# Gate and up of experts 3 to 6 as seven block products (Strassen and Winograd's scheme) in a fused attention and expert kernel

## The reference, cut to what matters

```
gate = einsum('btd,edf->ebtf', x, Wg)
up   = einsum('btd,edf->ebtf', x, Wu)
gate, up of the first two experts: plus a low-rank term
mid  = silu(gate) * up
out  = einsum('ebtf,efd->ebtd', mid, Wd)       (low-rank term for the first two)
y    = einsum('bte,ebtd->btd', weights, out)   (weights: a router over the 8 experts)
x    = x + gb * y
```

## Time and profile before

| | |
|---|---|
| time, median of 3 runs | 805.98 us (804.53 to 806.50) |
| the profiled execution's own time | 805.75 us |
| its span, first to last instruction | 804.0 us |
| mean granted clock of PE | 0.998 |
| busy: PE, DVE, ACT, POOL | 793.1, 508.3, 465.8, 403.3 us |
| instructions | 14773 |

### The profile page before, as it was taken

The page is one execution under the profiler, slowest core; times in us unless marked ns, Lnnn a source line. Parts: engine busy times, 40 slices in busy tenths (PEclk is TensorE's granted clock), DMA queues, the critical chain, the costliest instruction groups (busy, mean ns, idle before and its releaser), DMA issues.

```text
span 804.0 us, 14773 instructions
## 1 busy us (share of the span) xinstructions
PE 793.1 (99%) x5116; PEld 710.0 (88%) x5116; DVE 508.3 (63%) x1074; ACT 465.8 (58%) x1259; POOL 403.3 (50%) x547
## 2 busy tenths in 40 slices
PE   9899999999999999999999999999999999999997
PEld 8688899999999999999999999898888888888887
DVE  5667676475466667457557757666785454554575
ACT  5777677677577767767667866652553232332322
POOL 3767587486567567567657656220311010110493
PEclk9999999999999999999999999999999999999999
DMA  9200010000000000000000000202410110100002
GB/s 334 104 28 1 2 61 1 1 8 2 0 8 2 1 4 5 1 2 8 1 1 8 1 1 2 79 1 53 118 40 2 40 40 1 40 0 1 1 1 106
DMA packets 8329, 22.32 MB, mean 28 GB/s; under 512 B 1592, under 2 KB 4280, under 8 KB 8128
## 3 DMA queue, kind: packets, MB, share of 16 engines
q1 hardware_dynamic: 7680, 21.29, 7.9%
q10 hardware_dynamic: 576, 0.08, 0.1%
HBM read 19.26 MB, written 2.11 MB: 27 GB/s over the span
## 4 chain that ended last, share of the span: by engine, by line
PE 94%; DVE 2%; ACT 1%; issue 1%; POOL 1%; DMA 1%; ACTq 0%; DVEq 0%; POOLq 0%
PE ps_o L671 14%; PE ps_proj L548 9%; PE ps_proj L550 9%; PE ps_proj L549 9%; PE ps_s L548 7%; PE ps_s L549 7%; PE ps_s L550 7%; PE ps_turn L600 4%; PE ps_y L548 4%; PE ps_y L549 4%; PE ps_y L550 4%; PE ps_turn L618 3%; PE ps_turn L548 2%; PE ps_turn L549 2%; PE ps_turn L550 2%; PE ps_o L550 2%
## 5 line engine op out<-in xcount | busy, mean ns | idle before, releaser
L671 PE MATMUL ps_o<-vaug,probs 128*128 128x129 f32 x1024 | 136.1, 276 | 1.7 <-POOL probs L1674 0.9
L671 PEld LDWEIGHTS ps_o<-vaug,probs 128*128 128x128 f32 x1024 | 130.0, 192 | 8.0 <-POOL probs L1674 1.4
L993 ACT ACTIVATE ps_s<-ps_s,knorm 128x512 f32<-128x512 f32 x128 | 79.3, 657 | 96.2 <-PE ps_s L550 96.1
L1287 DVE RECIPROCAL rden<-ps_o 128x2 f32<-128x2 f32 x128 | 21.8, 170 | 155.5 <-PE ps_o L671 155.3
L1680 POOL TENSOR_TENSOR we_lo<-raw_e,we_hi 128x512 fp32r<-128x512 f32 x22 | 28.4, 1318 | 161.3 <-ACT we_hi L1036 161.3
L1257 DVE TENSOR_TENSOR prod<-ps_proj,cs 128x1024 f32<-128x1024 f32 x76 | 92.5, 1218 | 11.0 <-ACT sq L936 11.0
L1625 POOL TENSOR_TENSOR root<-ssq,powers 128x4 f32<-128x4 f32 x76 | 77.8, 1024 | 27.4 <-ACT sq L936 27.4
L936 ACT ACTIVATE sq<-ps_proj 128x128 f32<-128x128 f32 x304 | 80.1, 279 | 18.9 <-PE ps_proj L550 16.0
L1641 POOL TENSOR_TENSOR prod<-prod 128x512 f32<-128x512 f32 x62 | 80.1, 1292 | 10.0 <-DVE prod L1257 10.0
L548 PE MATMUL ps_proj<-w_hi,h_hi 128*128 128x512 f32 x192 | 83.3, 434 | 0.4 <-DVE h_lo L1204 0.4
L1672 POOL TENSOR_SCALAR_AFFINE_SELECT probs<-probs 128x256 f32<-128x256 f32 x64 | 26.4, 412 | 106.7 <-ACT probs L1001 106.4
(11 more groups left out here) (220 smaller groups left out, 2191.2 us busy)
## 6 DMA issues: line engine op xcount, KB each, us to landing
raw_e<-in_we SPq DMA_DIRECT2D x8, 768.0 KB, 4.4
raw_p<-in_wqkv SPq DMA_DIRECT2D x6, 512.0 KB, 8.5
raw_e<-in_wo SPq DMA_DIRECT2D x4, 512.0 KB, 12.7
x_all<-in_x SPq DMA_DIRECT2D x1, 1536.0 KB, 7.3
out<-acc SPq DMA_DIRECT2D x3, 512.0 KB, 2.6
x_all<-in_wmod SPq DMA_DIRECT2D x1, 1024.0 KB, 10.4
gates_a<-gate_rows_dram SPq DMA_DIRECT2D x8, 128.0 KB, 2.9
gates_b<-gate_rows_dram SPq DMA_DIRECT2D x1, 1024.0 KB, 10.2
```

The lines of the kernel that those rows point to most:

```text
L671: mm = pe.matmul(ps_o[:, h * (D + 1):(h + 1) * (D + 1)], probs[:, s % 2, at:at + P], vaug[b % 2][:, k, i // 2, :], start=(h == 0 and k == ...
L993: act.activation(ps_s[:, t, :], ps_s[:, t, :], ACT.Tanh, scale=knorm[:, b % 2, t, i // 2:i // 2 + 1]).then_inc(tanh_done, 1)
```

## The change

For experts 3 to 6 (tiles `SEVEN` = 12 to `EIGHT` - 1 = 27) gate and up are computed each as a 2x2 block product with seven products instead of eight. The blocks are the two halves of the 256 input features and of the 256 hidden features on the weights' side (A11, A12, A21, A22), and the two feature halves and the two halves of 256 tokens on the tokens' side (B11 ...). The sums of weight blocks (S) are made by POOL in place in `raw_e` (`sums_s`, four additions of 128x256), rounded by ACT (`round_s`) and their lower halves made by POOL (`rest_s`); the sums of token blocks (T) are made once per token group, the same way (`sums_t`, `round_t`, `rest_t`; `h2_dram` keeps the tokens of one group, whose place expert 1's weights take, in DRAM, from where they are read back).

PE's order in a tile is that of `seven(m)`. Gate and up stand side by side in one bank, so every product writes 2 x 256 columns. One bank (`chain`) gathers A11 B11, then + S2 T2, + S1 T1, + S4 B22, and is copied to `kept` by ACT in between (`keep` 0, 2, 3, and `keep` 1 for the second bank); the additions that make the quarters of gate and up are on DVE (`add_c11`, `add_c21`) and POOL (`add_c22`). The four pieces of the products with Wd of the tile before stand between the block products. `mid` is made by quarters (`product_sums`, `product_rest`), its halves rounded by `seven_head` and finished by `seven_tail` in the next tile. `EXPERT_STEPS` is spread: gate and up of an expert are split in the first tile of the one before, Wd in the tile ahead of its first. `part` gets a buffer for each group, some other tiles new places, and one low-rank step moves from tile 9 to tile 8. `sums_t(n)` is four POOL operations of 128x256, each waiting for the one before. The diff, cut to its core:

```diff
-LOW_STEPS = {NEXT + 1: [0, 1], NEXT + 2: [2], NEXT + 4: [3], NEXT + 5: [4, 5]}
-EXPERT_STEPS = {FIRST_OF[e] - 2: [(e, 0), (e, 1), (e, 2)] for e in range(3, NE)}
-EXPERT_STEPS |= {FIRST_OF[2] - 2: [(2, 0), (2, 1)], FIRST_OF[2] - 1: [(2, 2)]}
+LOW_STEPS = {NEXT + 1: [0, 1], NEXT + 2: [2], NEXT + 4: [3, 4], NEXT + 5: [5]}
...
+SEVEN, EIGHT = FIRST_OF[NL + 1], FIRST_OF[NE - 1]
...
+EXPERT_STEPS = {FIRST_OF[2] - 2: [(2, 0), (2, 1)], FIRST_OF[2] - 1: [(2, 2)], FIRST_OF[2] + 1: [(3, 0), (3, 1)], FIRST_OF[3] - 1: [(3, 2)]}
+EXPERT_STEPS |= {FIRST_OF[e - 1]: [(e, 0), (e, 1)] for e in range(NL + 2, NE)}
+EXPERT_STEPS |= {FIRST_OF[e] - 1: [(e, 2)] for e in range(NL + 2, NE)}
+
+SUMS_S = {FIRST_OF[e] - 3: e for e in range(NL + 1, NE - 1)}
+ROUND_S = {FIRST_OF[e] - 2: e for e in range(NL + 1, NE - 1)}
+REST_S = {FIRST_OF[e] - (1 if e == NL + 1 else 2): e for e in range(NL + 1, NE - 1)}
+
+SUMS_T = {SEVEN - 4: 2, SEVEN - 2: 3}
+ROUND_T = {SEVEN - 4: [0], SEVEN - 3: [1], SEVEN - 1: [2, 3]}
+REST_T = {SEVEN - 4: 0, SEVEN - 2: 1, SEVEN - 1: 2, SEVEN: 3}
+SLOT_SUMS = {63: 0, 64: 1}
...
+            sp.dma_start(h2_back[:], h2_dram).then_inc(h2_back_in, 16)
...
                 sp.wait_ge(we_split, 3 * (e - 1) - 2)
+                if e - 2 > NL:
+                    sp.wait_ge(s_split, sums_of(e - 2))
                 expert(e)
...
+            def seven(m):
+                e, n = TILES[m]
+                q = m - SEVEN
+                of = [blocks(m, w0) for w0 in (0, 2)]
+                chain, second_bank, third_bank = (ps_s[:, 0, :], ps_proj[:, 1, :])[q % 2], ps_s[:, 1, :], ps_proj[:, 0, :]
+
+                def both(dst, weights, moving, first=False):
+
+                    for n_of, names in enumerate(of):
+                        mm = product_of(dst[:, n_of * S:(n_of + 1) * S], names[weights], names[moving], first and n_of == 0)
+                    return mm
+
+                if m == FIRST_OF[e]:
+                    pe.wait_ge(we_split, 3 * e)
+                    pe.wait_ge(s_split, sums_of(e))
+                if m == SEVEN + n:
+                    pe.wait_ge(t_split, 2 * n + 2)
+                pe.wait_ge(mid_done, 2 * m - 2 if q else 2 * SEVEN - 1)
+                both(chain, "A11", "B11", True).then_inc(seven_ready, 1)
+                if q:
+                    pe.wait_ge(c21_added, q)
+                both(second_bank, "S3", "T3", True).then_inc(seven_ready, 1)
+                if q:
+                    pe.wait_ge(c11_added, q)
+                else:
+                    pe.wait_ge(mid_done, 2 * SEVEN)
+                both(third_bank, "A12", "B21", True).then_inc(gu_ready, 1)
+                pe.wait_ge(seven_copied, 4 * q + 1)
+                both(chain, "S2", "T2").then_inc(seven_ready, 1)
+                pe.wait_ge(seven_copied, 4 * q + 2)
+                both(second_bank, "A22", "-T4").then_inc(gu_ready, 1)
+                steps = [(2 * m - 2, 0), (2 * m - 2, 1), (2 * m - 1, 0), (2 * m - 1, 1)]
+                down(*steps[0])
+                pe.wait_ge(seven_copied, 4 * q + 3)
+                both(chain, "S1", "T1").then_inc(gu_ready, 1)
+                for step in steps[1:-1]:
+                    down(*step)
+                pe.wait_ge(seven_copied, 4 * q + 4)
+                both(chain, "S4", "B22").then_inc(gu_ready, 1)
+                down(*steps[-1])
...
+                if b // 2 == 2:
+                    act.dma_start(h2_dram[:, b % 2], h2f[b][:]).then_inc(h2_kept[b % 2], 16)
...
+            def round_s(e):
+                act.wait_ge(s_made, 4 * (e - NL))
+                if e == NL + 1:
+                    act.wait_ge(low_ready, 3 * NL)
+                else:
+                    act.wait_ge(gu_ready, 4 * LAST_OF[e - 2] + 4)
+                act.activation(s_hi[e % 2][:], raw_e[:, e % 2, 0:KT, :], ACT.Copy).then_inc(s_hi_done, 1)
+                act.activation(su_hi[e % 2][:], raw_e[:, e % 2, KT:2 * KT, :], ACT.Copy).then_inc(s_hi_done, 1)
+
...
+            def keep(m, n):
+
+                q = m - SEVEN
+                chain = (ps_s[:, 0, :], ps_proj[:, 1, :])[q % 2]
+                if q == 0:
+                    act.wait_ge(h2_turned, B)
+                    act.wait_ge(y_gated, B)
+                    act.wait_ge(low_ready, 3 * NL)
+                elif n == 0:
+                    act.wait_ge(c11_added, q)
+                elif n == 2:
+                    act.wait_ge(c21_added, q)
+                else:
+                    act.wait_ge(c22_added, 2 * q)
+                if n < 3:
+                    act.wait_ge(seven_ready, 3 * q + n + 1)
+                else:
+                    act.wait_ge(gu_ready, 4 * m + 3)
+                act.activation(kept[:, n].rearrange("p a n -> p (a n)"), ps_s[:, 1, :] if n == 1 else chain, ACT.Copy).then_inc(seven_copied, 1)
...
+            def silu_sums(m):
+
+                q = m - SEVEN
+                act.wait_ge(c11_added, q + 1)
+                act.wait_ge(c21_added, q + 1)
+                act.activation(quarters[:, 0, 0::2], quarters[:, 0, 0::2], ACT.Silu).then_inc(quarter_silu, 1)
+
+            def silu_rest(m):
+
+                q = m - SEVEN
+                act.wait_ge(c22_added, 2 * q + 1)
+                act.activation(quarters[:, 0, 3], quarters[:, 0, 3], ACT.Silu).then_inc(quarter_silu, 1)
+                act.wait_ge(gu_ready, 4 * m + 4)
+                act.wait_ge(mid_done, 2 * m)
+                chain = (ps_s[:, 0, :], ps_proj[:, 1, :])[q % 2]
+                act.activation(quarters[:, 0, 1], chain[:, 0:S], ACT.Silu).then_inc(quarter_silu, 1)
+
+            def seven_head(m, f):
+
+                act.wait_ge(mid_done, 2 * m + 2 - f)
+                act.wait_ge(down_ready, 2 * m - 2)
+                act.activation(mid_hi[:, m % 2, f, :], mid_seven[:, f, :], ACT.Copy).then_inc(mid_hi_done, 1)
...
+            for m in range(SEVEN, EIGHT):
+                if m > SEVEN:
+                    seven_head(m - 1, 1)
+                keep(m, 0)
+                if m > SEVEN:
+                    seven_head(m - 1, 0)
+                keep(m, 1)
+                keep(m, 2)
+                silu_sums(m)
+                keep(m, 3)
+                for e, m3 in EXPERT_STEPS.get(m, ()):
+                    split_e(e, m3)
+                if m in ROUND_S:
+                    round_s(ROUND_S[m])
+                silu_rest(m)
+            seven_head(EIGHT - 1, 1)
+            seven_head(EIGHT - 1, 0)
...
+            def add_c11(m):
+
+                q = m - SEVEN
+                dve.wait_ge(gu_ready, 4 * m + 1)
+                dve.wait_ge(seven_copied, 4 * q + 1)
+                if q:
+                    dve.wait_ge(half_product, q)
+                else:
+                    dve.wait_ge(mid_done, 2 * SEVEN)
+                    dve.wait_ge(mid_split, 2 * SEVEN)
+                dve.tensor_tensor(quarters[:, :, 0], ps_proj[:, 0, :].rearrange("p (a n) -> p a n", a=2), kept[:, 0], ALU.add).then_inc(c11_added, 1)
+
+            def add_c21(m):
+
+                q = m - SEVEN
+                dve.wait_ge(gu_ready, 4 * m + 2)
+                dve.wait_ge(seven_copied, 4 * q + 3)
+                dve.tensor_tensor(quarters[:, :, 2], ps_s[:, 1, :].rearrange("p (a n) -> p a n", a=2), kept[:, 2], ALU.add).then_inc(c21_added, 1)
+
+            def product_sums(m):
+
+                q = m - SEVEN
+                dve.wait_ge(quarter_silu, 3 * q + 1)
+                dve.wait_ge(mid_split, 2 * m)
+                dve.tensor_tensor(mid_seven[:, :, 0:S], quarters[:, 1, 0::2], quarters[:, 0, 0::2], ALU.mult).then_inc(half_product, 1)
...
+            def product_rest(m):
+
+                q = m - SEVEN
+                dve.wait_ge(quarter_silu, 3 * q + 2)
+                dve.wait_ge(c22_added, 2 * q + 2)
+                dve.wait_ge(half_product, q + 1)
+                dve.tensor_tensor(mid_seven[:, 1, S:], quarters[:, 1, 3], quarters[:, 0, 3], ALU.mult).then_inc(mid_done, 1)
+                dve.wait_ge(gu_ready, 4 * m + 4)
+                dve.wait_ge(quarter_silu, 3 * q + 3)
+                chain = (ps_s[:, 0, :], ps_proj[:, 1, :])[q % 2]
+                dve.tensor_tensor(mid_seven[:, 0, S:], chain[:, S:], quarters[:, 0, 1], ALU.mult).then_inc(mid_done, 1)
+
+            def seven_tail(m, f):
+                dve.wait_ge(mid_hi_done, 2 * m + 2 - f)
...
+            for m in range(SEVEN, EIGHT):
+                if m > SEVEN:
+                    seven_tail(m - 1, 1)
+                    seven_tail(m - 1, 0)
+                add_c11(m)
+                add_c21(m)
+                if m > SEVEN:
+                    accumulate(2 * m - 3)
+                product_sums(m)
+                accumulate(2 * m - 2)
+                product_rest(m)
+            seven_tail(EIGHT - 1, 1)
+            seven_tail(EIGHT - 1, 0)
+            accumulate(2 * EIGHT - 3)
...
+            def rest_t(n):
+                for b in range(2):
+                    pool.wait_ge(t_hi_done, 2 * n + b + 1)
```

(87 more changed lines are left out.)

124 lines of the change are left out of this document (108 added, 16 removed).

## The result

The changed kernel took 808.28 us (median; 806.78 to 809.87), the kernel before 805.23 us (804.53 to 807.64) beside it: ratio 1.0033, 95% interval 1.0026 to 1.0040. The change costs 3 us. The profiled execution of after took 809.87 us with a span of 808.0, that is 4.0 above the span of before.

The account below looks back on a forecast made before the run. PE, busy 99% of the span, was taken as the bound. -8.57 (stream) + 3.46 (wait) + 1.7 (clock) + 5.1 (transitions) + 0.2 (tile 8) = +1.9, giving 807.9 us; range 799 to 812.

Parts of the forecast that it names:

- stream of 16 tiles: PE in tiles 12 to 27: 66 matmuls of 0.119 us per tile, 125.66 instead of 134.23 us, so -8.57 us.
- first wait of tile 12: PE before tile 12 waits for POOL's low parts of expert 3's sums, starting at 632.39 instead of 628.93: +3.46 us.
- clock after it: After PE's idle stretch before tile 12 the granted clock drops for a while: +1.7 us, bounds 0 and 1.7.
- transitions: Between tiles, POOL's 512-element instruction behind c22 delays product_rest and so PE: ten times 0.51, +5.1 us, bounds 0 to 10.
- tile 8: sums_t(2) on POOL holds up DVE's small router operations against 2.2 us of slack: +0.2 us, bounds 0 and 1.0.
- Rival (4): PE in the block products is bound by loads, 0.19 us per matmul instead of 0.119: 844 us, chance 1%.
- The lock: POOL and two-SBUF-input DVE operations each wait for the other's whole instruction; product_rest ends late, PE 0.52 us late.
- what else is added: Extra POOL and ACT work before tile 12, moved low-rank step, DMAs, late output work: all 0 except +0.2 us at tile 8.
- (1): Rival: the lock does not reach PE, as product_rest slips in or the copies have more air: 802.8 us, chance 25%.
- (2): Rival: POOL's c22 additions, blocked by product_sums, are late by 0.2 us or more in every tile: 811.1 us, chance 15%.
- (3): Rival: full gain, tile 12's wait short or without clock cost, and no lock: 797.5 to 801 us, chance 12%.
- (5): Rival: the change leaves the kernel's time as it is, 806.0 us, chance 2%.

Follow-up runs that it names:

- changed_again: The changed kernel itself, unaltered, measured again beside the kernel before: 809.04 us, ratio 1.0047.
- sums_first: Against the changed kernel, POOL makes expert 3's low parts of the sums ahead of the last weight split before tile 12: 804.19 us, ratio 0.9985.
- tails_too: Changed kernel with POOL waiting for product_rest, low sums first, T sums behind the router, second subtractions behind mid_lo, last T's low part in two places: 796.01 us, ratio 0.9892.

## Why the prediction was right, and where it was not

It said 807.9 and the median is 808.28. The median rose by 3.05 us where +1.9 was forecast. The terms, against the profiled execution of after (+4.0 in the span; predicted +1.9):

| term | predicted | measured |
| --- | --- | --- |
| stream of 16 tiles | -8.57 | -9.6 (16 x 7.79 against 134.23) |
| first wait of tile 12 | +3.46 | +3.2 (start to start) |
| clock after it | +1.7 | +1.6 for tile 12 here (0.1 of it stays at full clock); no drop in four of eight profiled executions |
| transitions | 10 x 0.51 = +5.1 | +6.95 |
| tile 8 | +0.2 | +1.5 |
| from the first 12 us | 0 | +0.4 in this execution, nothing in changed_again |

- **The stream.** Right in kind; the size was 1 us too small. A matmul of 256 costs 0.118, not 0.119: I had divided 2.85 us of the part with Wd, which holds small hidden gaps. Rival (4), loads as the bound, fell with 7.79.
- **The first wait.** Right in its place, its chain and nearly in its size: ACT's rounding at 629.46, then three instructions of POOL of 1.25 to 1.29, the last into `su_lo`, then PE. The run sums_first shows the order as the cause.
- **The clock.** The size from the earlier trace rows fits nearly where it comes, 1.3 to 1.5. I took it as certain; it comes in half of the profiled executions. This is the main reason why the median stands only 3.05 above before and the profiled spans 4.0.
- **The lock.** The mechanism of the earlier trace rows holds, and three runs with 256, 512 and 1024 elements show it. PE's steps 4 and 5 of tile 15 start 2.26 and 3.27 us into the tile, where the prediction had 2.38 and 3.38. The nine transitions with one instruction of 512 and nothing else cost 0.51 to 0.59, on average 0.56 against 0.51. Two steps of the term were wrong. I had 0 for the three behind additions of 256, because `keep` 1 was to end in time; it was 0.27 each (0.8 in all): POOL's further additions run beside `mid_lo`, which I had not followed past `product_rest`. The row of the pair in tile 14 is 2.41 us, against 1.48 in the earlier trace rows; it ends at 655.93 and PE's product with Wd, which needs it, begins at 656.03:

```profile
653.52 2.41 DVE L1632 TENSOR_TENSOR mid_lo<-mid_seven,mid_hi 128x512 fp32r<-128x512 f32 x2 [0.37 <-ACT mid_hi L1242]
```

  And tile 13 lost 1.14: POOL's two subtractions for T of the last group, placed at m = 12, run beside `mid_lo` (the pair took 2.70 us). I had counted them as hidden under "what else is added".
- **Tile 8.** The mis-sized step. I measured the slack at the wrong reader: the product at 600.49 has 2.2 us until 602.68, but ahead of it stands the accumulation whose bank PE's product with Wd takes. In before it ended at 599.11 and PE went on at 599.25: hardly any slack. DVE and PE of the kernel before there:

```profile
598.23 0.88 DVE L1410 TENSOR_SCALAR acc<-ps_turn,r_wf 128x256 f32<-128x256 f32 x2
...
599.25 0.35 PE L548 MATMUL ps_turn<-we_hi,mid_hi 128*128 128x256 f32 x1
```

  And the operations that POOL holds included two TENSOR_SCALAR of 4 elements, with a single tensor as input, which I had said were spared. Together they lost 0.25 + 0.40 + 0.42 + 0.37 = 1.44 us.
- **The sum was better than its terms.** A stream 1 us too dear and a certain clock drop (0.8 too much for the median) stood against 1.85 and 1.3 that were missing. That the total came within 0.4 us is luck to that extent.
- **Rivals.** (1) was excluded by the idle of 1.23 us of ACT behind `product_rest` and by PE's starts. (2) did not hold: tiles 26 and 27 have additions for c22 too and lose nothing. (3) is what tails_too is: 796.0, below even the 797.5 of that case. (5) is excluded by the interval, whose lower end is 2 us above no change.
- **The signs.** Three came as said: the wait before tile 12 (3.0 us), the half clock behind it in this execution, and rows of `product_rest` of 1.44. The sign that tiles 25 and 26 take 7.85 was put one tile too early: m = 24 has a split behind c22, so tile 25 pays (8.34), and the free ones are 26 and 27.

On the two operations with one input the Trainium skill, "SBUF — State Buffer", section "Who interferes with whom", has the rule that I missed: `tensor_scalar` can enter a mode of DVE that takes the shared ports, and `tensor_reduce` cannot. The trace of tile 8 agrees: the two TENSOR_SCALAR took 0.42 and 0.54 instead of 0.17, and the two TENSOR_REDUCE, which also began beside POOL's additions, 0.19 as in the kernel before.

## What to carry to other kernels

When work goes to POOL, ask for each of its instructions which operation of DVE with two SBUF inputs comes next, and who waits for that; the price is the rest of POOL's instruction, not a share of it. A wait that holds POOL back until DVE's short operation is done, or an instruction cut in two, can be worth more than the work costs: here one line on POOL gave 4.4 us. And measure slack at every reader ahead in the queue of the engine that is delayed, not only at the one that the change is about.

## What the hardware showed that I had not expected

- DVE's 256-element product took 0.43, 0.89, 1.44 or 2.55 us behind nothing, 256, 512 or 1024 elements of POOL, within 0.02 us each time that it came about 0.1 us after POOL's instruction had begun.
- After an idle stretch of 3.0 us PE's granted clock fell in four of eight profiled executions (tile 12 at 0.82 to 0.84, 9.2 to 9.4 us instead of 7.9), and in none of the five without that stretch. What decides it, no run here tells.
- For matmuls of 256 columns it makes next to no difference which of the two weight buffers is read (in tails_too 7.78 to 7.80 us in tiles of the even experts, 7.73 to 7.85 in those of the odd, four tiles of either 31.2), while those of 512 took 0.233 us with the even experts' and 0.227 with the odd (24 in 5.45 us, tile 28 of after). The cause stays open.
